# Up projection of the second expert layer with streamed weights as the stationary operand

## What is computed

```python
probs = softmax(flat @ router_w.T)                 # 8 experts
topk_probs, topk_idx = top_k(probs, 2)             # each node goes to 2 of them
h1 = einsum('nc,ehc->neh', flat, w1)               # c = 128, h = 341
h3 = einsum('nc,ehc->neh', flat, w3)
h  = silu(h1) * h3
y  = einsum('neh,ech->nec', h, w2)
out = einsum('ne,nec->nc', gates, y)               # added to x
```

## Time and profile before

| | us |
|---|---|
| median of 3 runs (range) | 525.76 (522.95 to 525.88) |
| span of the profiled execution | 520.2 |
| median less span: what lies around it | 5.6 |
| PE busy in the span | 450.7 (87%) |
| DVE busy | 342.4 (66%) |
| ACT busy | 239.3 (46%) |

### The profile page before, as it was taken

How to read it: one execution, slowest core, us unless ns; L and a number is a source line. 1 busy time by engine, 2 the same in 40 slices (tenths; PEclk the granted TensorE clock), 3 DMA queues, 4 the chain that set the end, 5 groups by cost and what they waited for, 6 DMA issues and landing times.

```text
span 520.2 us, 6589 instructions
## 1 busy us (share of the span) xinstructions
PE 450.7 (87%) x1892; PEld 268.2 (52%) x1892; DVE 342.4 (66%) x753; ACT 239.3 (46%) x390; POOL 69.8 (13%) x115
## 2 busy tenths in 40 slices
PE   4588598977698998998979999999988878999996
PEld 2533454544355664454644444444444556787875
DVE  0997979787648772225773887787577655744572
ACT  4987789577777552104134031222213036644441
POOL 5000000000011000000000000100600502564442
PEclk9679788989989999999999999999989999999999
DMA  8889500000000000000000000530100111122422
GB/s 282 275 265 372 238 0 0 0 1 1 0 2 1 0 2 0 1 0 3 1 0 0 1 0 31 184 111 20 45 6 1 48 43 44 53 68 64 123 68 84
DMA packets 27006, 31.70 MB, mean 61 GB/s; under 512 B 3490, under 2 KB 20591, under 8 KB 26967
## 3 DMA queue, kind: packets, MB, share of 16 engines
q1 hardware_dynamic: 25111, 27.71, 16.8%
q0 software_dynamic: 1856, 3.51, 2.0%
HBM read 19.44 MB, written 11.77 MB: 60 GB/s over the span
## 4 chain that ended last, share of the span: by engine, by line
PE 53%; DVE 25%; ACT 11%; issue 9%; POOL 1%; DVEq 0%; POOLq 0%; ACTq 0%
PE bank L1340 9%; PE bank L1149 4%; PE bank L1422 4%; PE bank L1406 4%; PE bank L1288 4%; PE bank L1407 3%; DVE pr_ring L2074 3%; PE bank L1110 2%; DVE y_units L1551 2%; PE bank L1329 2%; DVE y_units L1562 2%; PE bank L999 2%; PE bank L1413 2%; DVE hr_ring L1877 2%; DVE t_units L1557 2%
## 5 line engine op out<-in xcount | busy, mean ns | idle before, releaser
L1340 PE MATMUL bank<-pr_ring,hW 128*128 128x512 f32 (+3 forms) x198 | 94.1, 560 | 6.1 <-DVE pr_ring L2074 5.4
L2074 DVE SCALAR_TENSOR_TENSOR pr_ring<-adjT,regR,bank 128x512 f32<-128x512 f32 (+3 forms) x99 | 64.7, 680 | 35.5 <-PE bank L1329 34.0
L1340 PEld LDWEIGHTS bank<-pr_ring,hW 128*128 128x128 f32 (+1 forms) x198 | 34.4, 193 | 35.3 <-DVE pr_ring L2074 18.4
L999 PE MATMUL bank<-y_units,msg 128*128 128x512 f32 (+3 forms) x66 | 34.4, 652 | 15.1 <-DVE y_units L1572 15.0
L1110 PE MATMUL bank<-hr_ring,W2s 128*128 128x512 f32 (+1 forms) x96 | 45.3, 560 | 0.0
L1877 DVE TENSOR_TENSOR hr_ring<-hr_ring,bank 128x512 f32<-128x512 f32 (+1 forms) x48 | 29.5, 619 | 20.9 <-ACT hr_ring L796 14.9
L585 POOL DMA_INDIRECT yg<-pr_ring,goes x32 | 31.2, 976 | 50.9 <-DVE pr_ring L2113 49.0
L796 ACT ACTIVATE hr_ring<-bank,b1c 128x512 f32<-128x512 f32 (+1 forms) x48 | 29.8, 628 | 15.7 <-PE bank L972 15.7
L970 PE MATMUL bank<-zhi,W1hi 128*128 128x512 f32 (+1 forms) x48 | 35.1, 731 | 0.3 <-DVE zlo L1546 0.3
L2125 DVE TENSOR_TENSOR hbuf<-hbuf,bank 128x341 f32<-128x341 f32 x36 | 18.3, 508 | 23.9 <-PE bank L1407 21.1
L579 POOL DMA_INDIRECT xg<-rowx,slot x22 | 22.3, 1013 | 69.6 <-DVE slot L1684 63.5
(11 more groups left out here) (321 smaller groups left out, 889.9 us busy)
## 6 DMA issues: line engine op xcount, KB each, us to landing
xg<-zeros SPq DMA_DIRECT2D x1, 3575.0 KB
xg<-zeros SPq DMA_DIRECT2D x1, 3055.0 KB
wall<-in_w SPq DMA_DIRECT2D x2, 1364.0 KB
adjT<-in_adjT SPq DMA_DIRECT2D x1, 2560.0 KB
xblk<-xg SPq DMA_DIRECT2D x36, 65.0 KB
adjT<-in_adjT SPq DMA_DIRECT2D x1, 1650.0 KB
adjT<-in_adjT SPq DMA_DIRECT2D x3, 512.0 KB, 5.9
adjT<-in_adjT SPq DMA_DIRECT2D x1, 1024.0 KB
```

The costliest lines, as they stand in the source:

```text
L999: mm = nc.tensor.matmul(B_GNN[:, 0:w], msg[0:r, j, :], y_units[0:r, g % RINGY, i, 0:w], start=(j == 0), stop=(j == T - 1))
L1340: nc.tensor.matmul(B_ACC[:, 0:w], hW[0:r, j, k * P:(k + 1) * P], ring[0:r, 0:w], start=(k == 0 and j == 0), stop=(k == K - 1 and j == T - ...
L2074: nc.vector.scalar_tensor_tensor(out=pr_ring[0:r, 4 + p % R_RING, 0:w], in0=adjT[0:r, j, cols(c)], scalar=g_col[0:r, j, k:k + 1], in1=B_F[ ...
```

## The change

- `wall` keeps only the down weights (three slices of 128 columns an expert). The up weights of w1 and w3 are laid in DRAM, expert by expert, as 128 rows of 684 numbers (2736 bytes; 350 KB in all), and SP loads those of each block anew into `wring`, a ring of four (`up_load`). For that SP reads one more number a block, `up_row`, which DVE writes.
- `up` swaps the operands: a slice of 114 weight columns is stationary, x^T (128 columns) streams. Six matmuls instead of two, and the result comes out turned, hidden x rows, three slices of 128 columns side by side. Silu and multiply now work on 114 x 384 instead of 128 x 341.
- `hidden_turned` goes, on PE and on ACT. `down(b - 1)` now stands in PE's turn b, and `block_out(b - 1)` in DVE's, one turn earlier than before. `down` waits for the multiply (`m_set`) instead of the ACT copy (`ht_set`).
- Three semaphores are merged into neighbours (`sel16_set`, `ln_log`), and one small memset goes.

```diff
+            def up_load(b):
+                at(sp, "h3_ps", b - WRING + 1)
+                row = sp.value_load(up_row[0:1, b:b + 1], min_val=0, max_val=(E - 1) * P)
+                sp.dma_start(wring[:, b % WRING, :], w13_d[bass.ds(row, P), :]).then_inc(s[f"w_in{b % WRING}"], 16)
+            block_load(0)
+            block_load(1)
             for b in range(NB):
-                block_load(b)
+                if b == BLOCKS[0]:
+                    sp.wait_ge(s["list_set"], 2)
+                up_load(b)
+                if b + 2 < NB:
+                    block_load(b + 2)
                 if b == FETCH:
...
-            def up(b, base):
+            def up(b):
+                at(pe, f"w_in{b % WRING}", 16 * (b // WRING + 1))
                 at(pe, "xt_set", b + 1)
                 at(pe, "m_set", b if b < ALONE else b - 1)
...
-                nc.tensor.matmul(B_H1[pair(b)][:, 0:H1], x, walls[:, bass.ds(base, H1)], start=True, stop=True).then_inc(s["h1_ps"], 1)
-                nc.tensor.matmul(B_H3[pair(b)][:, 0:H1], x, walls[:, bass.ds(base + H1, H1)], start=True, stop=True).then_inc(s["h3_ps"], 1)
-            def hidden_turned(b):
+                for k in range(3):
+                    mm = nc.tensor.matmul(B_H1[pair(b)][0:HP, k * P:(k + 1) * P], wring[:, b % WRING, k * HP:(k + 1) * HP], x, start=True, stop=True)
+                mm.then_inc(s["h1_ps"], 1)
+                for k in range(3, 6):
+                    mm = nc.tensor.matmul(B_H3[pair(b)][0:HP, (k - 3) * P:(k - 2) * P], wring[:, b % WRING, k * HP:(k + 1) * HP], x, start=True, stop=True)
+                mm.then_inc(s["h3_ps"], 1)
+            def down(b, base):
                 at(pe, "m_set", b + 1)
-                at(pe, "ht_set", b)
-                for k in range(3):
-                    mm = nc.tensor.transpose(B_HT[0:HP, k * P:(k + 1) * P], hbuf[:, b % 2, k * HP:(k + 1) * HP], ident[:, :])
-                mm.then_inc(s["ht_ps"], 1)
-            def down(b, base):
-                at(pe, "ht_set", b + 1)
                 at(pe, "y_set", b)
...
                     if b + 2 < NB:
                         block_turned(b + 2)
                     if b:
-                        hidden_turned(b - 1)
-                    if b > 1:
-                        down(b - 2, bases.pop(b - 2))
+                        down(b - 1, bases.pop(b - 1))
...
                 join(NB - 4)
-                hidden_turned(NB - 1)
-                down(NB - 2, bases.pop(NB - 2))
                 join(NB - 3)
                 down(NB - 1, bases.pop(NB - 1))
```

More of the change, by code:

```diff
@@ L26 @@
 HT = [(k * HP, min(HP, H1 - k * HP)) for k in range(3)]
-WALL = 2 * H1 + len(HT) * P
+WW = 2 * len(HT) * HP
+WRING = 4
 GROUPS = [(0, 6), (6, T)]
@@ L255, in build @@
         ])
-        (y_units, msg, zhi, zlo, masks, wc, s_sum, wall, rowx, before, oneb, slot) = place("slotB", 43648, [
+        (y_units, msg, zhi, zlo, masks, wc, s_sum, wall, wring, rowx, before, oneb, slot) = place("slotB", 43648, [
             [("y_units", [P, RINGY, 2, CW], F32), ("msg", [P, T, P], F32), ("zhi", [P, 2, CW], F32R), ("zlo", [P, 2, CW], F32R)],
             [("masks", [P, T, N], BF16), ("wc", [P, T, PARTS, K * BUCKETS], BF16), ("s_sum", [P, T, K * BUCKETS], F32)],
-            [("wall", [P, E, WALL], F32), ("rowx", [P, OWN, 2, XW], F32), ("before", [P, P], BF16), ("oneb", [P, 2], BF16), ("slot", [P, T, 2], U32)],
+            [("wall", [P, E, len(HT) * P], F32), ("wring", [P, WRING, WW], F32), ("rowx", [P, OWN, 2, XW], F32), ("before", [P, P], BF16), ("oneb", [P, 2], BF16), ("slot", [P, T, 2], U32)],
         ])
-        (W1hi, W1lo, W2s, hr_ring, GT0, Wl0, Wg, wcat, gWT, b2x, b2hi, b2lo, nsT, ge, pr_ring, xblk, xturned, hbuf, hturned, mk, ecap, bno, cmp, shares1,
-         place1, t1, floor1, chosen, spot, place_no, red1, row_no, wall_at, unused, goes) = place("slotC", 46144, [
+        (W1hi, W1lo, W2s, hr_ring, GT0, Wl0, Wg, wcat, gWT, b2x, b2hi, b2lo, nsT, ge, pr_ring, xblk, xturned, hbuf, mk, ecap, bno, cmp, shares1,
+         place1, t1, floor1, chosen, spot, place_no, red1, row_no, wall_at, up_row, unused, goes) = place("slotC", 46144, [
             [("W1hi", [P, E, H0], F32R), ("W1lo", [P, E, H0], F32R), ("W2s", [P, E, M0, P], F32),
@@ L627, in ln_rsqrt @@
                 at(act, "ln_var", n + 1)
-                nc.scalar.activation(v, ln_bank(l, c)[:, 0:w], ACT.Ln, bias=eps[:, 0:1]).then_inc(s["ln_log"], 1)
-                at(act, "ln_log", n + 1)
+                nc.scalar.activation(v, ln_bank(l, c)[:, 0:w], ACT.Ln, bias=eps[:, 0:1]).then_inc(s["ln_y0"], 1)
+                at(act, "ln_y0", 2 * n + 1)
                 nc.scalar.activation(y, v, ACT.Exp, scale=-0.5).then_inc(s["ln_y0"], 1)
-                at(act, "ln_y0", n + 1)
+                at(act, "ln_y0", 2 * n + 2)
                 nc.scalar.activation(v, y, ACT.Square).then_inc(s["ln_y2"], 1)
@@ L902, in support @@
                 nc.scalar.copy(ES[c][:, 0:width(c)], B_ACC[:, 0:width(c)]).then_inc(s["es_set"], 1)
-            def hidden_turned(b):
-                at(act, "ht_ps", b + 1)
-                at(act, "y_ps", b - 1)
-                nc.scalar.copy(hturned[0:HP, b % 2, :], B_HT[0:HP, 0:3 * P]).then_inc(s["ht_set"], 1)
             def experts():
@@ L915, in experts @@
                     at(act, "h1_ps", b + 1)
-                    at(act, "ht_ps", b - 1)
-                    nc.scalar.activation(hbuf[:, b % 2, 0:H1], B_H1[pair(b)][:, 0:H1], ACT.Silu).then_inc(s["s_silu"], 1)
+                    at(act, "y_ps", b - 1)
+                    nc.scalar.activation(hbuf[0:HP, b % 2, :], B_H1[pair(b)][0:HP, 0:3 * P], ACT.Silu).then_inc(s["s_silu"], 1)
                     for task in ACT1A.get(b, []):
                         gat_side(task)
-                    if b:
-                        hidden_turned(b - 1)
                     for task in ACT1B.get(b, []):
                         gat_side(task)
-                hidden_turned(NB - 1)
             act.wait_ge(s["flag_set"], 2)
@@ L1421, in down @@
                 for k, (_, r) in enumerate(HT):
-                    mm = nc.tensor.matmul(B_Y[:, 0:P], hturned[0:r, b % 2, k * P:(k + 1) * P],
-                                          walls[0:r, bass.ds(base + 2 * H1 + k * P, P)], start=(k == 0), stop=(k == 2))
+                    mm = nc.tensor.matmul(B_Y[:, 0:P], hbuf[0:r, b % 2, k * P:(k + 1) * P],
+                                          walls[0:r, bass.ds(base + k * P, P)], start=(k == 0), stop=(k == 2))
                 mm.then_inc(s["y_ps"], 1)
@@ L1709, in route_list @@
                                                op0=ALU.mult, op1=ALU.add)
-                nc.vector.tensor_scalar(wall_at[0:1, first:first + nb], expert, E - 1.0, float(WALL), ALU.min, ALU.mult).then_inc(s["list_set"], 1)
+                nc.vector.tensor_scalar(up_row[0:1, first:first + nb], expert, E - 1.0, float(P), ALU.min, ALU.mult)
+                nc.vector.tensor_scalar(wall_at[0:1, first:first + nb], expert, E - 1.0, float(len(HT) * P), ALU.min, ALU.mult).then_inc(s["list_set"], 1)
             def route(n):
@@ L2129, in experts @@
                         gat_side(task)
-                    if b > 1:
-                        block_out(b - 2)
+                    if b:
+                        block_out(b - 1)
                     for task in DVE1B.get(b, []):
@@ L2135, in experts @@
                         block_places(DVE_PLACE[b])
-                for b in (NB - 2, NB - 1):
-                    block_out(b)
+                block_out(NB - 1)
                 finish()
@@ L2254, in cols3, with rows13 @@
         return b.reshape(3, 128).transpose(1, 0)
+    def rows13(w1, w3):
+        both = _np.zeros((E, P, 2, WW // 2), w1.dtype)
+        both[:, :, 0, 0:H1] = w1.transpose(0, 2, 1)
+        both[:, :, 1, 0:H1] = w3.transpose(0, 2, 1)
+        return both.reshape(E * P, WW)
     laid = {
@@ L2279 @@
         "rw": g["L1_ffn_router_w"].transpose(1, 0),
-        "w1": g["L1_ffn_w1"].transpose(2, 0, 1).reshape(128, -1),
-        "w3": g["L1_ffn_w3"].transpose(2, 0, 1).reshape(128, -1),
+        "w13": rows13(g["L1_ffn_w1"], g["L1_ffn_w3"]),
         "w2": g["L1_ffn_w2"].transpose(0, 2, 1).reshape(-1, 128),
```

39 lines of the change are left out of this document (16 added, 23 removed).

## The result

Twelve executions each: 526.42 us median (524.34 to 528.49) for the changed kernel, 524.26 (522.16 to 526.96) for the one before. Ratio 1.0043, interval 1.0023 to 1.0064: slower by 0.4%, some 2.2 us, where I had forecast 1.8 less. It lies inside the range and within the 1% that the chances called the same, but on the wrong side of zero.

The account below looks back on a forecast made before the run. PE's own work was taken to bound 22 blocks, chains over DVE and ACT blocks 0 to 12. Terms -3.1 - 0.3 + 2.4 - 0.8 = -1.8 us gave 524.0 us against 525.76, range 519.5 to 529.5.

Parts of the forecast that it names:

- Blocks that PE bounds: 22 mid-stage blocks: longer up, no transposes, a block takes 2.12 us instead of 2.26; -3.1 us.
- as cheap as up per column: Bound on the new up's 12 matmuls: at the old up's price per column, a block takes 0.04 us less still.
- rival of the open weight loads: Up's weight loads beside nothing: 3.6 us a block, 36 blocks +49, 575 us; chance 0.02.
- Blocks 0 to 12: Early blocks: start +0.5, new wait making T(3) +1.4, later gains -1.1 and -0.55; sum -0.3 us, between -1.5 and +0.8.
- SP and the fetch: SP's two loads a block take 2.28 us against PE's 2.12, and the fetch leaves later; +2.4 us.
- The ring alone doesn't stall PE: Weight ring: 3.2 us in hand at block 13, falling 0.16 a block, 2.0 gone by turn 29; no stall.
- Landed at 2.9: A 350 KB weight load lands 2.9 us after issue, between 192 KB (2.4) and 677 KB (3.7).
- +2.4, which cover the 1.7 of the late weights: Around turn 30: DVE's wait for the fetch stalls PE 2.4 us, hiding block 30's weights, late by some 1.7.
- no lag: Lower bound on PE's stall from the late fetch, if SP doesn't fall behind: +0.3 us.
- DMA traffic itself: hidden: Streaming 350 KB in 2.12 us adds 165 GB/s to 81, engines' share being 0.29; no cost.
- SP becomes the bound: Rival: weights' issue costs 0.65 us, SP's turn 2.5, lead gone after 8 blocks; +3.6 us, 529.4; chance 0.18.
- The end: After T(35): down(33) already done, two transpose sets gone, PE's joins end last; -0.8 us, between -1.3 and 0.

Follow-up runs that it names:

- e13_best: e12_late_x5 with block 0's weights asked for ahead of its rows, and turn 2's mean matmul ahead of down(1); ratio 0.9979 to the kernel before.
- e1_fetch: The changed kernel with SP fetching the first group's rows two turns earlier, its place before the change; ratio 1.0037 to the kernel before.
- e4_issue: The changed kernel with only 16 columns of each weight load after the first four blocks (result differs); ratio 0.9996 to the kernel before.
- e14_x_late: e13_best with SP issuing the loads of x up to block 17 again and ACT only from block 18 on; ratio 0.9979 to the kernel before.
- e7_fetch_act: The changed kernel with the fetch of the first group's rows issued by ACT in its turn 24 instead of SP; ratio 1.0002 to the kernel before.
- e2_nostream: The changed kernel without up weight loads after the first four blocks (result differs); ratio 0.9947 to the kernel before.
- e11_late: The changed kernel with the first group's fetch after the loop over the blocks and its addition in the last turn; ratio 1.0011 to the kernel before.
- e12_late_x5: e11_late with the loads of x from block 5 on issued by ACT, five blocks ahead; ratio 0.9957 to the kernel before.

## Why the prediction was wrong

The forecast of -1.8 us is -0.3 for blocks 0 to 12, -0.3 for 13 to 32, -0.4 for 32 to 35 and -0.8 for the end. The two profiled executions give +0.8, +2.6, -0.5 and, with what follows the first addition, +0.3, together +3.2. So over half of the difference lies in turns 13 to 32. That the time fell inside the range is not to the forecast's credit: the sign was wrong, and the range was wide enough for both.

**The base.** I took what lies around the span as 5.6 us, median less span. In the executions that give both numbers the difference is 1.7 to 2.5. The profiled execution of before was therefore itself one of about 522. The difference between forecast and before doesn't hang on this.

**Blocks that PE bounds** (2.26 to 2.12, -3.1): right, and a little more: 2.09, which over 22 blocks is -3.7. My bound "as cheap as up per column" was the closer one. The rival of the open weight loads is gone with it: turns of 2.09, not 3.6. The Trainium skill (TensorE: Matmul & The Clock Gate, The mechanism) says in one sentence that a weight load overlaps only when the row group differs, and in another that it may also go ahead into the background weight buffer. All stationary operands here are 113 to 128 rows high, so that none has rows of the array for itself, and they overlap: the measurement decides against the first sentence for this kernel, and no row shows whether the second is what happens.

**Blocks 0 to 12.** Start +0.5: measured 2.72 us from the last graph instructions to T(0) where it was 2.15, +0.57. Right in size. Turn 2: T(3) at +1.4; measured 0.57 + 1.16 = +1.7, near my upper bound, 1.8. The wait is there, 1.54 us, but putting the mean matmul ahead of it gave only 0.2: down(1) and the transpose then stand between the mean matmul and up(3), 1.71 us in e13_best (426.94 to 428.65) where it was 1.00 (426.04 to 427.04). The gain of -1.65 from block 3 to 13 came as -0.92 in this execution and as -1.4 to -1.5 where the clock stayed full from 418 to 457 us (e1_fetch, e4_issue, e14_x_late); it was 0.96 in this one.

**SP and the fetch: the step that failed.** Three of its numbers:
- "The ring alone doesn't stall PE." SP's floor is 2.26 us a turn (2.28 forecast), but from block 17 to 24 the issues of the weights went from 460.98 to 478.64, 2.52 a turn; with 16 columns a load it was 2.40. So a lead of 3.2 shrank by 0.43 a block, not 0.16, and by turn 24 it was gone. Of the 1.8 us that these seven turns take beyond the floor, 0.7 are SP's wait for the second group's table, ahead of the rows of block 19 (in SP's waits `SPq L394 <- DMA xg<-rowx,slot: 0.7, 1, 0.7`), and 0.6 are six reads of a number from SBUF that took 0.34 to 0.40 us instead of 0.27, between 465.5 and 472.2. In e4_issue one issue took 0.86 us instead of 0.33. Why single reads and issues are longer no run shows.
- "Landed at 2.9." The row for `wring` says 3.5 in the median, 2.8 to 5.1, with the engines' share at 0.78. The 2.8 us that the prediction works out from the Trainium skill (DMA: Bandwidth & Descriptors, Anatomy of one DMA) are an estimate, and the section gives its formula for DMAs that GpSimd issues, while SyncE issues these. The shortest landing seen agrees with it, but it is no price for a load in this crowd.
- "+2.4, which cover the 1.7 of the late weights." Turns 29 to 32 take 3.36 more than before, 4.3 more than without waits. The fetch left at T(25) + 7.4 (forecast + 6.0), and DVE could add at + 13.4 (forecast + 11.2). The two waits are there as described, but one doesn't cover the other: taking DVE's away (e1_fetch, e7_fetch_act) leaves PE waiting for weights. Even without streamed weights turns 29 to 32 take 7.34 us (e2_nostream), 1.1 more than without waits, where the bound "no lag" said 0.3.

From block 13 to 32 my steps make 19 x -0.14 + 2.4 = -0.3 us; measured -0.95 + 0.16 + 3.36 = +2.6.

**"DMA traffic itself: hidden."** Not so. It makes weights, rows, fetch and scatters land later (e4_issue against after: 1.8 us in turns 13 to 29, 0.7 in the tail). The rival "SP becomes the bound" named this direction with 2.5 us a turn and a loss of 7.8; the rate was met for seven blocks only and not by its cause (SP's issue of the weights stayed at 0.33 us, not 0.65), the loss was 6.2 against no waits.

**The end** (-0.8): came as 0.0. PE's joins were to end last; POOL did, because the scatters' landing went from 2.7 to 3.9 us and delayed the last fetch. Where that wait is gone the tail is 7.39, 1.2 less than before: PE's part was sized rightly (-1.14), and what I had wrong is that POOL would end earlier.

**What is shown and what not.** Shown: the loss of turns 29 to 32 comes from the late fetch and the loads behind it (it goes when the fetch stands last, e11_late), that of 13 to 29 from two loads a turn with landings made longer by the bytes (it goes without the bytes, e4_issue, and with one load a turn, e12_late_x5). With the fetch last and one load a block moved off SP's list, the kernel with all its bytes comes out 0.4% faster than before (e12_late_x5), the two that refine it 0.2%, not distinguishable from no change. Their own medians are 522.13, 522.48 and 522.63 us; much of what sets the 0.4% apart is the median of the kernel before, 524.26 us beside the first and 523.14 and 523.01 beside the others. Not reached: a kernel with all the repairs and no new wait. By the best stages of the last three kernels it would take 93.7 us from T(0) where e12_late_x5 takes 96.0; no run shows it.

## What to carry to other kernels

A load that is issued once a block by an engine with a fixed price per issue is a pipeline stage of its own: put its turn (here 2.26 us for two loads) beside the bound engine's (2.09) before counting the bytes, and follow the lead block by block with the landing times of the traffic that the change itself creates. A large transfer placed in such a list delays what is issued behind it (landings of 5.0 to 5.1 us for 3.5), and issued on another engine's queue it delayed the loads as well (6.2 us, e7_fetch_act); it belongs after the last load that has a deadline. And moving an issue to another engine moves the wait into that engine's list: look at what stands behind it there.
